# A graph kernel's layer loop: seven-tile chunks over two PSUM banks in place of halves in one bank

## The reference

```python
for i in range(3):
    msg = relu(x[src] + edge_attr)                 # 200000 x 128
    aggr = segment_sum(msg, dst, num_segments=6250)
    h = (x + aggr) @ W1[i] + b1[i]
    h = relu(bn(h, g_mlp[i], be_mlp[i]))
    h = bn(h @ W2[i] + b2[i], g_out[i], be_out[i])
    x = relu(h) if i != 2 else h
```

## Time and profile before

| | |
|---|---|
| median of three runs | 5063.85 us (5047.44 to 5081.66) |
| span of the profiled execution | 4090.3 us |
| the rest of the median, outside the span | 973.5 us |
| PE busy | 3879.3 us (95%) |
| DVE busy | 3556.7 us (87%) |
| ACT busy | 3072.5 us (75%) |
| POOL busy | 2859.0 us (70%) |
| mean granted TensorE clock | 0.958 |
| layer loops, first to last window added | 1871.4 to 2592.5, 2672.5 to 3319.1, 3396.5 to 4044.2 us |

### The profile page before, as it was taken

One profiled execution on the slowest core, in us unless ns is written; L12 is line 12 of the kernel. 1 busy time (PEld: TensorE's weight loads), 2 busy tenths in 40 slices (PEclk: granted clock), 3 DMA queues, 4 the chain that ended last, 5 costly groups with the idle time before them and its releaser, 6 DMA issues.

```text
span 4090.3 us, 151537 instructions
## 1 busy us (share of the span) xinstructions
PE 3879.3 (95%) x50507; PEld 3753.5 (92%) x50510; DVE 3556.7 (87%) x6832; ACT 3072.5 (75%) x7847; POOL 2859.0 (70%) x2594
## 2 busy tenths in 40 slices
PE   3899997999999999989999999899999989999998
PEld 3899996999999999979999999699999969999996
DVE  7799985777777777779999999799999989999997
ACT  4799994677777777777777777678888867887886
POOL 0288885777777777756777777277777736777773
PEclk7788888999999999999999999899999999999999
DMA  9989889998888888868999999589999958999995
GB/s 140 216 291 305 286 277 297 234 248 253 247 250 250 253 247 250 247 211 293 337 338 334 333 329 333 171 300 310 323 310 318 317 176 288 318 319 311 314 316 186
DMA packets 710002, 1132.45 MB, mean 277 GB/s; under 512 B 157402, under 2 KB 535084, under 8 KB 709564
## 3 DMA queue, kind: packets, MB, share of 16 engines
q1 hardware_dynamic: 493068, 787.26, 57.5%
q10 hardware_dynamic: 133200, 176.14, 17.7%
q0 software_dynamic: 83552, 166.66, 12.7%
HBM read 883.83 MB, written 246.33 MB: 276 GB/s over the span
## 4 chain that ended last, share of the span: by engine, by line
PE 84%; DVE 5%; DMA 3%; issue 2%; ACT 2%; SPq 2%; POOL 1%; ACTq 0%; DVEq 0%; PEld 0%; POOLq 0%
PE ps L2049 20%; PE ps L1955 15%; PE ps L2073 14%; PE ps L1942 12%; PE ps L2097 7%; PE ps L2076 4%; PE ps L1883 2%; PE ps L1903 2%; PE ps L1904 2%; PE ps L1891 2%; DMA unit_x<-gin_rows,unit_src 2%; PE ps L2144 2%; PE ps L2087 1%; POOL unit_x L941 1%; DMA h_rows<-att 1%
## 5 line engine op out<-in xcount | busy, mean ns | idle before, releaser
L941 POOL DMA_INDIRECT unit_x<-gin_rows,unit_src x1449 | 1446.6, 998 | 487.8 <-issue 318.4
L878 POOL DMA_INDIRECT attr_by_slot<-abuf,ridx x1020 | 1286.0, 1261 | 455.9 <-issue 308.5
L2049 PE MATMUL ps<-x_parts,src_turned 128*128 128x128 bf16 x15876 | 1137.0, 222 | 21.5 <-ACT ps L1158 18.5
L2049 PEld LDWEIGHTS ps<-x_parts,src_turned 128*128 128x128 fp8e4 x15876 | 948.6, 99 | 67.8 <-issue 25.3
L1158 ACT ACTIVATE ps<-sums 128x512 f32<-128x512 f32 x1512 | 825.8, 546 | 125.9 <-DVE all_split_msg L1692 70.7
L1066 ACT ACTIVATE val<-ps,val 128x128 f32<-128x128 f32 x2597 | 717.9, 375 | 182.6 <-DVE val L1519 182.6
L1685 DVE TENSOR_TENSOR dst_hot<-ps,dl_slot 128x896 fp32r<-128x896 f32 x756 | 817.8, 1082 | 3.5 <-issue 0.4
L1955 PE MATMUL ps<-val,src_hot 128*128 128x129 f32 x5194 | 691.6, 282 | 3.0 <-ACT val L1066 2.5
L2073 PE MATMUL ps<-all_split_msg,dst_hot 128*128 128x256 f32 x3528 | 648.8, 304 | 13.2 <-DVE all_split_msg L1692 12.6
L1166 ACT ACTIVATE all_split_msg<-ps 128x512 fp32r<-128x512 f32 x1008 | 543.7, 539 | 146.0 <-PE ps L2049 113.7
L1692 DVE SCALAR_TENSOR_TENSOR all_split_msg<-ps,all_split_msg 128x512 fp32r<-128x512 f32 x1008 | 609.1, 617 | 14.0 <-ACT all_split_msg L1166 11.5
(11 more groups left out here) (268 smaller groups left out, 5787.5 us busy)
## 6 DMA issues: line engine op xcount, KB each, us to landing
sums<-attr_by_slot SPq DMA_DIRECT2D x756, 448.0 KB
turned_hot<-rows_by_block ACTq DMA_DIRECT2D x392, 384.0 KB
attr_by_slot<-zeros SPq DMA_DIRECT2D x36, 3136.0 KB
unit_attr<-in_edge_attr SPq DMA_DIRECT2D x204, 448.0 KB
abuf<-in_edge_attr SPq DMA_DIRECT2D x68, 960.0 KB
src_turned<-src_hots SPq DMA_DIRECT2D x504, 112.0 KB
src_row<-rows_by_group SPq DMA_DIRECT2D x252, 112.0 KB
src_hots<-src_turned SPq DMA_DIRECT2D x252, 112.0 KB
```

The lines of the kernel that those rows point to most:

```text
L878: pool.indirect_dma_start(out=attr_table, out_offset=bass.IndirectOffsetOnAxis(ap=ridx[:, g, t0 + t:t0 + t + 1], axis=0), in_=abuf[:, k % ...
L941: pool.indirect_dma_start(out=unit_x[:, half_place(k), t, :], out_offset=None, in_=gin_rows[n], in_offset=bass.IndirectOffsetOnAxis(ap=uni ...
L2049: ins = pe.matmul(ps[:, BANK[h], k * D:(k + 1) * D], src_turned[:, b * P:(b + 1) * P], x_parts[:, part, b, :], start=False, stop=(k == til ...
```

## The change

All that worked on halves works on whole chunks of 896 floats in each partition, except PE's sums, which keep their halves as places in the order. Three pairs of PSUM banks (`PAIR`) take the place of five single banks. Two chunks are gathered and seeded ahead (`G_LEAD = 2`) in place of three halves. Seeds, messages and rests are one instruction to a chunk, 128x896. Waits and counts go by chunk. The row of counting numbers for the targets is no longer in PSUM: it is read from the tile `iota_one` in SBUF. In layer 1, chunks 0, 1, 3, 5 and 6 are split, in place of 0, 2, 4 and 6. ACT's places for the units' ReLUs and the kept window are renumbered to chunks.

```diff
-BANK = (4, 2, 3, 0, 1, 2, 3, 4, 0, 1, 2, 3, 0, 1)
-IOTA_BANK = 5
+PAIR = (0, 1, 2, 0, 1, 2, 1)
...
-G_LEAD = 3
-AHEAD = ((3, 4), ()) + tuple((h + G_LEAD,) for h in range(2, G_HALVES))
-SEED_LEAD = 3
+G_LEAD = 2
...
-RELU_AT = {6: 0, 13: 1}
+RELU_AT = {3: 0, 6: 1}
...
-WINDOW_OUT_AT = 2
+WINDOW_OUT_AT = 1
...
-SPLITS = ((0, 2, 4, 6), (0, 1, 2, 3, 4, 5, 6), (0, 1, 2, 3, 4, 5, 6))
-SPLIT_PLACES = ({0: 0, 2: 1, 4: 0, 6: 1},) + 2 * ({0: 0, 1: 1, 2: 2, 3: 0, 4: 1, 5: 2, 6: 1},)
-WHOLE_PLACES = ({1: 0, 3: 1, 5: 0}, {}, {})
+SPLITS = ((0, 1, 3, 5, 6), (0, 1, 2, 3, 4, 5, 6), (0, 1, 2, 3, 4, 5, 6))
+SPLIT_PLACES = ({0: 0, 1: 1, 3: 0, 5: 0, 6: 1},) + 2 * ({0: 0, 1: 1, 2: 2, 3: 0, 4: 1, 5: 2, 6: 1},)
+WHOLE_PLACES = ({2: 0, 4: 1}, {}, {})
...
+        def chunk_ps(c):
+            return ps[:, 2 * PAIR[c]:2 * PAIR[c] + 2, :].rearrange("p b e -> p (b e)")[:, 0:G_TILES * D]
...
+                def seed(i, c):
+                    act.wait_ge(s_attr[c], 16 * (n * BUCKETS + i + 1 + cleared(c)))
+                    before = pair_user(c)
                     if not (isinstance(i, int) and i == 0 and before < 0):
+                        if before % G_CHUNKS in SPLITS[n]:
                             act.wait_ge(s_low, lows_done(n, i, before))
                         else:
+                            act.wait_ge(s_msg, chunks_done + G_CHUNKS * i + before + 1)
+                    act.activation(chunk_ps(c), attr[:, parts_of(c), :].rearrange("p b d -> p (b d)"), ACT.Copy).then_inc(s_seed, 1)
+                def message(i, c):
+                    act.wait_ge(s_gath, chunks_done + G_CHUNKS * i + c + 1 + G_CHUNKS)
+                    act.wait_ge(s_used, halves_before + G_HALVES * i + 2 * place_user(n, c) + 2 + G_HALVES)
...
+                    act.activation(to.rearrange("p b d -> p (b d)"), chunk_ps(c), ACT.Relu).then_inc(s_msg, 1)
...
+                        message(i, c)
+                        if c == WINDOW_OUT_AT and not (isinstance(i, int) and i == 0):
                             keep_window(i - 1)
+                        if c + G_LEAD < G_CHUNKS:
+                            seed(i, c + G_LEAD)
                         elif more:
+                            seed(i + 1, c + G_LEAD - G_CHUNKS)
...
-                    vec.tensor_tensor(dst_hot[:, HOT[c], :, :], iota_ps.unsqueeze(1).to_broadcast([P, G_TILES, P]),
+                    vec.tensor_tensor(dst_hot[:, HOT[c], :, :], iota_one[:, :].unsqueeze(1).to_broadcast([P, G_TILES, P]),
...
+                def split_message(i, c):
+                    vec.wait_ge(s_msg, chunks_done + G_CHUNKS * i + c + 1)
+                    hi, low_of = (split_msgs[n][:, SPLIT_PLACES[n][c], k, :, :].rearrange("p b d -> p (b d)") for k in range(2))
+                    vec.scalar_tensor_tensor(low_of, chunk_ps(c), 0.0, hi, ALU.max, ALU.subtract).then_inc(s_low, 1)
...
-                    vec.tensor_tensor(unit_hot[:, half_place(k), 0:tiles, :], iota_ps[:, 0:U_WINDOW].unsqueeze(1).to_broadcast([P, tiles, U_WINDOW]),
+                    vec.tensor_tensor(unit_hot[:, half_place(k), 0:tiles, :], iota_one[:, 0:U_WINDOW].unsqueeze(1).to_broadcast([P, tiles, U_WINDOW]),
...
-                        if c in SPLITS[n]:
-                            split_message(i, h)
+                        if h % 2 == 0 and c in SPLITS[n]:
+                            split_message(i, c)
...
-                        for k in AHEAD[h]:
-                            if k < G_HALVES:
-                                gather(i, k)
-                            elif more:
-                                gather(i + 1, k - G_HALVES)
+                        if h % 2 == 0 and h // 2 + G_LEAD < G_CHUNKS:
+                            gather(i, h // 2 + G_LEAD)
+                        elif h % 2 == 0 and more:
+                            gather(i + 1, h // 2 + G_LEAD - G_CHUNKS)
                         sum_half(i, h)
```

More of the change, by code:

```diff
@@ L92, in since @@
     return [next(d for d in range(1, n + 1) if places[(k - d) % n] == places[k]) for k in range(n)]
-BANK_SINCE, HOT_SINCE = since(BANK), since(HOT)
-G_LEAD = 3
-AHEAD = ((3, 4), ()) + tuple((h + G_LEAD,) for h in range(2, G_HALVES))
-SEED_LEAD = 3
+PAIR_SINCE, HOT_SINCE = since(PAIR), since(HOT)
+G_LEAD = 2
 FIRST = 4
@@ L160 @@
 PACE, PACE_AHEAD = 2, 10
-LEFT_GROUP, LEFT_HALF = 1, 8
+LEFT_GROUP, LEFT_CHUNK = 1, 4
 LEFT_TILE = 7
@@ L512, in half_of, with pair_user, lows_done @@
             return c * G_TILES + (FIRST if second else 0), G_TILES - FIRST if second else FIRST
[L514 to L522, removed]
+        def pair_user(c):
+            return c - PAIR_SINCE[c]
+        def lows_done(n, i, c):
+            group, c = (i, c) if c >= 0 else (i - 1, c + G_CHUNKS)
+            return sum(BUCKETS * len(m) for m in SPLITS[:n]) + len(SPLITS[n]) * group + SPLITS[n].index(c) + 1
         def normed(eng, c):
@@ L1144, in _ @@
             for n in range(LAYERS):
[L1145 to L1152, removed]
+                halves_before, chunks_done = n * BUCKETS * G_HALVES, n * BUCKETS * G_CHUNKS
+                def seed(i, c):
+                    act.wait_ge(s_attr[c], 16 * (n * BUCKETS + i + 1 + cleared(c)))
+                    before = pair_user(c)
@@ L1206, in _ @@
                     act.wait_ge(s_copied_odd, ODD_BEFORE + CHUNKS - EVEN_TURNS)
-                for h in range(SEED_LEAD):
-                    seed(0, h)
+                for c in range(G_LEAD):
+                    seed(0, c)
                 group_of(0, True, parts=True)
@@ L2045, in gather @@
                     pe.sem_inc(s_go, 1)
-                    for k in range(tiles):
-                        b = first + k
+                    for k in range(G_TILES):
+                        b = c * G_TILES + k
+                        to = ps[:, 2 * PAIR[c] + k // BY_CHUNK, k % BY_CHUNK * D:(k % BY_CHUNK + 1) * D]
                         for part in range(PARTS):
-                            ins = pe.matmul(ps[:, BANK[h], k * D:(k + 1) * D], src_turned[:, b * P:(b + 1) * P], x_parts[:, part, b, :],
-                                            start=False, stop=(k == tiles - 1 and part == PARTS - 1), skip_group_check=True)
+                            ins = pe.matmul(to, src_turned[:, b * P:(b + 1) * P], x_parts[:, part, b, :],
+                                            start=False, stop=(k in (FIRST - 1, G_TILES - 1) and part == PARTS - 1), skip_group_check=True)
@@ L2121, in group_of @@
                             sum_unit(i, unit_at(SUM_AT, i, h))
-                for h in range(G_LEAD):
-                    gather(0, h)
+                for c in range(G_LEAD):
+                    gather(0, c)
                 group_of(0, True)
```

79 lines of the change are left out of this document (30 added, 49 removed).

## The result

| | before | changed |
|---|---|---|
| median of four runs | 5061.52 us | 5334.45 us |
| ratio, 95% interval | | 1.0524 [1.0476, 1.0572] |
| span of the profiled execution | 4090.3 us | 5337.8 us |

The time rose by 273 us, where 299 was forecast (5363 us). One of the changed kernel's four runs was a slow one of 12627.39 us; it is not in the ratio, and the median of the other three is 5329.51 us.

A forecast was written before the change was run, and what follows sets the result against it. The prediction took PE, and in layer 1 POOL as well, to bound the kernel. It added 202 (loop, layers 2 and 3), 90 (POOL) and 7 us (layer 1's loop), 299 in all, to 5063.85: 5363 us, range 5210 to 5540.

The forecast's parts named there:

- what lies around the span: Whole run: 973.5 us between profiled span and median of the runs, left alone and carried unchanged into the forecast.
- the sentence after the sum: Whole run: were the difference of span and median a slower execution throughout, the 299 us would be 370.
- The two-chunk lead loop: Layers 2 and 3: seeds wait for DVE's whole-chunk rests, PE for seeds; period 21.3 us for 18.33, +202 us.
- third rival: All layers: loop, POOL and granted clock halved after PE's pauses, 1.5 us more a group; 5521 us, chance 0.12.
- The counting numbers and POOL: Layer 1: DVE operations with two SBUF inputs delay POOL's gathers; period 23.7 us, +90 us, and +7 from the loop.
- The balance that left POOL no slack: Layer 1: 14 gathers and 2 late scatters need 20.9 us of POOL, about the period of 20.7 us.
- the 23.7 that POOL was reckoned to need: Layer 1: POOL's period in us with gathers delayed by DVE's SBUF reads; +3.0 us in each of 30 periods.
- the 123.1: Layer 1: us standing before 404 POOL gathers, counted as needed time, giving 1.30 us a gather.
- second rival: Loop alone, POOL's delay costing nothing; layer 1 goes to 21.8 us; +242, 5306 us, chance 0.13.
- PE's 0.75 us from the fifth split: Layer 1: one more split chunk takes about 0.75 us off PE's work a group, a gain gone in the loop.
- Larger operations at nothing: 128x896 operations save DVE half a microsecond and ACT over 1 us a group; ACT's gain, off the bound, worth nothing.

The follow-up runs named there:

- a_keep: The changed kernel with only the first unit's window moved behind the rest of chunk 6 in DVE's order; ratio 1.011 to the kernel before.
- a_add: The changed kernel with only the second unit's addition moved behind the rest of chunk 6 in DVE's order; ratio 1.0273 to the kernel before.
- a_warm: The changed kernel with 32 extra unused matmuls on PE ahead of the gathers of chunk 6 and the next chunk 1; ratio 1.033 to the kernel before.
- the control: The kernel before, unchanged, run again with a profile of its own; ratio 1.0006, span 5062.7 us.
- a_rest_first: The changed kernel with first unit's window and second unit's addition both behind the rest of chunk 6 on DVE; ratio 1.0132 to the kernel before, 5063 us.
- b_iota23: The kernel before with the counting numbers read from SBUF in layers 2 and 3 alone; ratio 1.0018 to the kernel before.

## Why the prediction was right, point by point

- **The baseline (what lies around the span): wrong in kind.** The 973.5 us were no time outside the span but a slower execution throughout, as the sentence after the sum allowed for. Every period that the prediction started from (18.33 and 20.71 us) was 5 us short of the timed ones, and the forecast periods with them (21.3 us in layers 2 and 3, where 26.5 came; PE busy 82% for 86%). That the difference came out so near is in part luck. Taken as it stands, the forecast loop of 21.3 us is shorter than the 23.3 us that a group already took, and would have cost nothing there. The loop of the runs was 5 us longer as well (26.5), by PE's piece at the lower clock and by DVE's waits, neither of which is in the sum. The other way, by the sentence after the sum, the forecast would have been 370 us, 97 too many. The parts missed in opposite directions: 18 us too few in layers 2 and 3, 42 too many in layer 1.
- **The two-chunk lead loop: right in mechanism, and in total by other terms.** +202 us forecast for layers 2 and 3, +220 measured (111.2 and 108.7). Its links stand in the chain, and a_keep and a_add open it. PE waits for ACT's seed twice a group, and ACT's seeds for DVE's rests, as forecast. Its size came out by another sum: the sum put the whole 3.0 us on the loop's work at full clock, which is worth a quarter to a third of the loss by the traces of a_warm and about a half by its timed ratio.
- **The slower clock (third rival, chance 0.12): it did come.** It was priced at 1.5 us a group on top of the loop. In layers 2 and 3 PE's own work is 1.8 us longer, and the traces of a_warm give back 2.1 to 2.4 of the 3.1 to 3.2 us. It was set against the loop, while it is part of it: the waits lower the clock, and the slower gather, sums and unit lengthen the loop that causes the waits. In timed ratios it is 1.9 of 5.2 points, some 97 us, so its share of the 220 us lies somewhere between 45% and 75%.
- **The counting numbers and POOL: half right.** The gathers grew as forecast, to 1116 ns in 700 us of layer 1 (986 in the control); whether that cost the changed kernel any time is not shown. But layer 1 did not become POOL's: no wait of DVE's unit addition for gathered rows is listed there, POOL is busy 516 of 800 us in the window row of layer 1 above, and waits for PE. The balance that left POOL no slack was that of the quicker execution; at 25.6 us a group (896.2 / 35) the 23.7 that POOL was reckoned to need fit in. It also counted 30.4 us of waits for PE, in the 123.1, as time that POOL needs. Forecast +97 for layer 1, measured +54.6, nearer to the second rival, the loop alone (+40); moving DVE's two steps takes most of it back (a_rest_first), while the clock alone does not (a_warm). The Trainium skill, "SBUF — State Buffer", § Who interferes with whom, infers that a VectorE operation with two SBUF inputs doesn't hold up descriptor generation; b_iota23's gathers are held up, 1139 ns for 988, as in the earlier trace rows. Whether it is their descriptors or the reading of their row numbers (`unit_src`, in SBUF) that waits, no run here shows.
- **PE's 0.75 us from the fifth split: worth nothing**, as forecast (1.0013 and 1.055).
- **Larger operations at nothing**: the prices held (rest 1.08 to 1.09 us, seed 0.92), and no saving shows.

## What to carry to other kernels

When buffers grow and their number falls, write down the loop from a buffer's release to its next use through every engine's fixed order; an engine's wait for something else that stands inside that loop (here DVE's wait for a unit's sum) is the first thing to move. A pause of PE costs more than its length where the work behind it runs at the lower clock, so test a suspected loop with cheap filler matmuls as well as with a changed order. Before adding a difference to a median, look whether the profiled execution took the time of the timed ones.

## What the runs showed of the hardware that was not expected

- The same program ran with a span of 4090.3 and of 5062.7 us. In the longer execution ACT took up a finished gather 2.55 us after its end, in the shorter one 0.52 us. Over all 1512 messages the median from the end of the gather to the start of the message is 2.2 us and 0.3 us. What makes PE's results late was not found.
- The granted clock was still 1.00 while PE stood (1.69 us busy in 4), and 0.63 in the 4 us after, when PE worked again: in this stretch the price of a pause fell on the work behind it.
